# A fused conv, graph-attention and mixture-of-experts block: node degrees from a one-hot histogram, more experts and row trips ahead of the node groups

## The reference

```python
h = (x_flat @ W_gat).reshape(M, HEADS, NUM_EXPERTS)
e = leaky_relu(a_src[src] + a_dst[dst]); e_max = segment_max(e, dst)
ee = exp(e - e_max[dst]); denom = segment_sum(ee, dst)
agg = segment_sum(h[src] * (ee / denom[dst])[:, :, None], dst)
scores = layernorm(agg + b_gat).reshape(M, HEADS, NUM_EXPERTS).mean(1)
```

## Time and profile before

| | us |
|---|---|
| median of 3 runs | 2300.75 (2294.5 to 2301.59) |
| span of the profiled execution | 2297.5 |
| PE busy | 1086.1 (47%) |
| DVE busy | 1594.7 (69%) |
| ACT busy | 762.8 (33%) |
| POOL busy | 1212.5 (53%) |
| mean granted TensorE clock | 0.720 of full speed |

### The profile page before, as it was taken

How to read it: one execution, slowest core, us unless ns; L and a number is a source line. 1 busy time by engine, 2 the same in 40 slices (tenths; PEclk the granted TensorE clock), 3 DMA queues, 4 the chain that set the end, 5 groups by cost and what they waited for, 6 DMA issues and landing times. The chain is left out here.

```text
span 2297.5 us, 16425 instructions
## 1 busy us (share of the span) xinstructions
PE 1086.1 (47%) x4821; PEld 479.8 (21%) x4821; DVE 1594.7 (69%) x3100; ACT 762.8 (33%) x1260; POOL 1212.5 (53%) x1233
## 2 busy tenths in 40 slices
PE   3897878778678887000700102433342425333330
PEld 1233343334533333000300001111111112111110
DVE  6999999995726999999209504364758384747658
ACT  4664846535345554000300002222232324222221
POOL 2000000000066777777777764777777777777771
PEclk8898878787589999555855556766676768676665
DMA  8202031021454322111221611344453535363543
GB/s 297 115 1 74 1 8 38 1 8 39 47 57 110 79 71 71 14 15 29 48 41 29 43 16 41 98 144 121 121 176 85 165 92 176 72 187 73 169 113 100
DMA packets 185735, 182.76 MB, mean 80 GB/s; under 512 B 81580, under 2 KB 164462, under 8 KB 176046
## 3 DMA queue, kind: packets, MB, share of 16 engines
q1 hardware_dynamic: 99262, 88.84, 14.4%
q0 software_dynamic: 43936, 47.85, 12.4%
q10 hardware_dynamic: 42448, 45.04, 6.4%
HBM read 105.23 MB, written 76.40 MB: 79 GB/s over the span
## 5 line engine op out<-in xcount | busy, mean ns | idle before, releaser
L519 POOL DMA_INDIRECT KC<-node_dram,KB x1026 | 1018.4, 993 | 938.8 <-DMA node_dram<-node_out 626.3
L740 PE MATMUL hidden_out<-XT,W 128*128 128x512 f32 x512 | 291.3, 675 | 540.8 <-ACT ARENA_A L956 539.9
L745 PE MATMUL hidden_out<-ARENA_A,W 128*128 128x512 f32 x512 | 264.7, 642 | 24.9 <-ACT ARENA_A L956 24.9
L956 ACT ACTIVATE ARENA_A<-hidden_out,b1c 128x512 f32<-128x512 f32 x256 | 174.2, 687 | 294.5 <-PE hidden_out L740 293.9
L740 PEld LDWEIGHTS hidden_out<-XT,W 128*128 128x128 f32 x512 | 97.3, 211 | 689.5 <-ACT ARENA_A L956 570.1
L1523 DVE TENSOR_TENSOR KB<-XG,MB 128x3072 bf16<-128x3072 f32 x20 | 67.1, 3354 | 163.5 <-DMA XG<-rest_dram,win_i 100.7
L1649 DVE TENSOR_SCALAR KB<-MB 128x16 f32<-128x16 f32 (+1 forms) x33 | 5.7, 172 | 238.3 <-DMA KC<-payload,slot_idx 126.8
L1800 DVE SCALAR_TENSOR_TENSOR XG<-XT,KB,XG 128x128 f32<-128x128 f32 x512 | 144.3, 347 | 14.9 <-DMA XT<-ye_dram 11.2
L959 ACT ACTIVATE ARENA_A<-hidden_out,b2c 128x512 f32<-128x512 f32 x128 | 87.9, 687 | 185.5 <-PE hidden_out L745 185.5
L1026 ACT ACTIVATE TA<-KB 128x400 f32<-128x400 f32 x32 | 16.2, 507 | 373.3 <-DVE KB L1656 373.2
L745 PEld LDWEIGHTS hidden_out<-ARENA_A,W 128*128 128x128 f32 x512 | 98.3, 207 | 182.4 <-ACT ARENA_A L956 103.1
(11 more groups left out here) (401 smaller groups left out, 2232.0 us busy)
## 6 DMA issues: line engine op xcount, KB each, us to landing
ye_dram<-ARENA_D ACTq DMA_DIRECT2D x32, 1024.0 KB, 4.0
XT<-ye_dram SPq DMA_DIRECT2D x32, 1024.0 KB, 13.5
KC<-node_dram,KB POOLq DMA_INDIRECT x1026
payload<-XT SPq DMA_DIRECT2D x1, 11520.0 KB
payload<-KC SPq DMA_DIRECT2D x115, 90.0 KB, 1.8
XG<-x_dram SPq DMA_DIRECT2D x32, 256.0 KB, 11.3
out_dram<-XG ACTq DMA_DIRECT2D x32, 256.0 KB, 3.4
KA<-in_L_ffn_edge_index_dram SPq DMA_DIRECT2D x1, 2048.0 KB, 9.0
```

The source lines that it names most:

```text
L519: pool.indirect_dma_start(row_buf[h][:, t, :], None, node_dram, bass.IndirectOffsetOnAxis(ap=KB[:, col:col + 1].bitcast(I32), axis=0)).the ...
L740: last = pe.matmul(PF[i % 2][:, :], W1[:, m // 2, (m % 2) * P:(m % 2) * P + P], XT[:, n * CHUNK:(n + 1) * CHUNK], start=True, stop=True)
L745: last = pe.matmul(PF[i % 2][:, :], W2[:, 2 * m + kk, :], HH[:, 2 * m + kk, :], start=kk == 0, stop=kk == 1)
L956: act.activation(HH[:, m, :], PF[i % 2][:, :], ACT.Gelu, bias=b1c[:, m:m + 1]).then_inc(S["hid_out"], 1)
```

## The change

- Windows, pivots, boundaries and the storing of the lists go. `split_digits` writes each key's destination as two bfloat16 digits (node number modulo 128, and divided by 128), each twice side by side. `one_hots` compares eight columns of keys at a time with `node_iota`, a bfloat16 row in SBUF, in pairs of equal neighbours: 144 batches for list 0 (one comparison of 8 x 128 and one of 8 x 256 elements each) and 144 for list 1 (two of 8 x 128). Four buffers. TensorE adds eight products of 128 x 128 by 128 x 256 (list 1: by 128 x 128) per batch into one PSUM bank: the degrees of all nodes, with no start positions. The starts are prefix sums of the degrees (two small matmuls and a scan).
- `pick_rest` stops at the picked keys; list 1 is not sorted across partitions any more. `drop_counted` raises its keys that are not ordinary edges out of the valid range, and the rest region now begins behind list 0.
- TensorE's batches stand between the expert layers by `HOT_PLAN`: 9 batches, then three ahead of each of the 16 steps of chunks 0, 1, 2 (list 0), none in chunks 3 and 4, three ahead of each step of chunks 5, 6, 7 (list 1). 28 chunks stand ahead of the node groups. On ScalarE the exponentials of the start-up come after chunk 12, those of the rest loop after chunk 22.
- POOL: 62 early trips, the rest loop, 10 more early trips, the catch-up loop, the loop for long lists, and 42 spread trips among the node groups. 114 trips as before.

```diff
-FIRST_TRIPS = 5
-MID_TRIPS = 42
-EARLY_TRIPS = 54
+EARLY_TRIPS = 72
+REST_AFTER = 62
-SPREAD_TRIPS = 60
+SPREAD_TRIPS = 42
-AHEAD, COUNTING = 14, 2
-FIRST_CHUNKS = AHEAD + COUNTING
+FIRST_CHUNKS = 28
+HOT_BUFS, HOT_AHEAD = 4, 9
+HOT_PLAN = ((0, 3), (0, 3), (0, 3), None, None, (1, 3), (1, 3), (1, 3))
+COUNTED, STORE_REST_AT, INIT_AT, REST_AT = len(HOT_PLAN), 6, 12, 22
...
-            for trip in range(FIRST_TRIPS):
+            for trip in range(REST_AFTER):
                 gather_rows(trip)
-            gather_windows(0)
-            for trip in range(FIRST_TRIPS, MID_TRIPS):
-                gather_rows(trip)
-            gather_windows(1)
-            for trip in range(MID_TRIPS, EARLY_TRIPS):
+            steps = rest_steps(pool)
+            first = pool.value_load(rest_steps_i[0:1, 1:2], min_val=0, max_val=REST_KEYS - 1)
+            with pool.Fori(0, steps) as i:
+                fetch_rest(i, first)
+            for trip in range(REST_AFTER, EARLY_TRIPS):
                 gather_rows(trip)
...
+            def count_nodes(a, count):
+                for n in islice(batches[a], count):
+                    real = n < HOT_BATCHES
+                    pe.wait_ge(S["hot_ready"], n + 1)
+                    for t in range(HOT):
+                        last = pe.matmul(H if real else H[:, P:], hot_p[n % HOT_BUFS][:, t, :],
+                                         hot_l[n % HOT_BUFS][:, t, 0 if real else P:],
+                                         start=n == 0 and t == 0, stop=n == LISTS * HOT_BATCHES - 1 and t == HOT - 1,
+                                         skip_group_check=True)
+                    last.then_inc(S["hot_used"], 1)
...
+            def split_digits(a):
+                keys = half(KA, a).bitcast(I32)
+                link(ts(digit_i, keys, SRC_BITS, P - 1, ALU.logical_shift_right, ALU.bitwise_and))
+                link(cp(digits_p, bc(digit_i, 2, [P, LROW, 2])))
+                link(ts(digit_i, keys, SRC_BITS + 7, None, ALU.logical_shift_right))
+                link(ts(digits_l, bc(digit_i, 2, [P, LROW, 2]), float(-(KEY_BIAS // P)), None, ALU.add))
+            def one_hots(a):
+                pairs = lambda ap: ap.rearrange("p t (n e) -> p t n e", e=2)
+                for b in range(HOT_BATCHES):
+                    n = a * HOT_BATCHES + b
+                    if n >= HOT_BUFS:
+                        dve.wait_ge(S["hot_used"], n - HOT_BUFS + 1)
+                    cols = slice(b * HOT, (b + 1) * HOT)
+                    for hot, digits, low, high in ((hot_p, digits_p, 0, P), (hot_l, digits_l, (0, P)[a], 2 * P)):
+                        shape = [P, HOT, (high - low) // 2, 2]
+                        last = tt(pairs(hot[n % HOT_BUFS][:, :, low:high]),
+                                  bc(node_iota[:, low:high].rearrange("p (n e) -> p n e", e=2), 1, shape),
+                                  bc(digits[:, cols, :], 2, shape), ALU.is_equal)
+                    last.then_inc(S["hot_ready"], 1)
+                dve.wait_ge(S["hot_ready"], (a + 1) * HOT_BATCHES)
```

More of the change, by code:

```diff
@@ L733, in _, with experts @@
             last_chunk()
-            def experts(n):
+            batches = [iter(range(a * HOT_BATCHES, (a + 1) * HOT_BATCHES)) for a in range(LISTS)]
+            def count_nodes(a, count):
[8 more added lines that the diff above has]
+                    last.then_inc(S["hot_used"], 1)
+            def experts(n, beside=None):
                 done = n * len(LAYERS)
                 for i, (layer, m) in enumerate(LAYERS):
+                    if beside:
+                        count_nodes(*beside)
                     if layer == 1:
@@ L794, in _ @@
-            last.then_inc(S["boundary_ready"], 1)
+                count_nodes(a, HOT_BATCHES)
             pe.wait_ge(S["degree_ready"], 1)
-            pe.transpose(TA[0][:, 0:P], starts[:, 0, 0:P], ident[:, :])
-            pe.transpose(TA[0][:, P:2 * P], degree[:, 0, :], ident[:, :])
-            pe.transpose(TA[1][:, 0:P], degree[:, 1, :], ident[:, :]).then_inc(S["starts_turned"], 1)
+            pe.matmul(TA[0][:, 0:P], before[:, :], degree_t[:, :], start=True, stop=True)
+            pe.matmul(TA[0][:, P:2 * P], ones[:, :], degree_t[:, :], start=True, stop=True).then_inc(S["starts_summed"], 1)
@@ L1333, in quadrant_step, with sort_keys @@
                 link(stt(keys, copy, -1.0, frm, ALU.mult, ALU.min))
-            def sort_keys(which):
-                keys, copy, other = (half(k, which) for k in (KA, KB, KC))
+            def sort_keys():
+                keys, copy, other = (half(k, 0) for k in (KA, KB, KC))
                 def times_sign(col, frm=keys):
                     link(ts(keys, frm, signs[:, col:col + 1], None, ALU.mult))
-                if which:
-                    yield from row_steps(keys, other, copy)
                 for m in range(1, LEVELS + 1):
                     if m <= 4:
-                        if m > 1 or which:
+                        if m > 1:
                             times_sign(m - 1, other)
@@ new lines, in drop_counted @@
+            def drop_counted():
+                keys, flags = half(KA, 1), KC[:, 1896:1896 + LROW]
+                link(ts(flags, keys, key_bits_as_float(REAL_END), key_bits_as_float(VALID_END), ALU.is_ge, ALU.mult))
+                tt(keys, keys, flags, ALU.max).then_inc(S["rest_placed"], 1)
+            sources()
+            dve.wait_ge(S["node_out_done"], CHUNKS * GROUPS)
+            dve.wait_ge(x1_stored[3], 16 * len(x_parts[3]))
+            dve.wait_ge(S["y_ready"], NORMS)
+            link(cp(node_iota, iota_f[:, :]))
@@ new lines, in _ @@
+            split_digits(0)
+            one_hots(0)
+            sort_steps(ROW, 1)
+            split_digits(1)
+            drop_counted()
+            one_hots(1)
+            dve.wait_ge(S["hot_used"], LISTS * HOT_BATCHES)
+            cp(degree_t[:, :], H[:, 0:P]).then_inc(S["degree_ready"], 1)
+            cp(last_degree[:, :], H[:, P:])
+            dve.wait_ge(S["degree_ready"], 1)
+            red(hist_tot[:, 0:1], degree_t[:, :], AX.X, ALU.max)
+            dve.wait_ge(S["starts_summed"], 1)
```

311 lines of the change are left out of this document (61 added, 250 removed).

## The result

| | before | after |
|---|---|---|
| median of 4 runs each, us | 2298.25 (2294.5 to 2301.59) | 2263.55 (2261.97 to 2266.61) |
| span of the profiled execution | 2297.5 | 2262.1 |
| PE, DVE, POOL busy | 1086.1, 1594.7, 1212.5 | 1252.2, 1617.5, 1210.5 |
| mean granted TensorE clock | 0.720 | 0.792 |

The median before is now that of four runs; the forecast was made from three. The ratio is 0.9849, with a 95% interval from 0.9835 to 0.9864: 1.5% faster. The forecast was 2262 us. The order of reading is the same as before: POOL's waits first (waiter, releaser, us, times, longest).

What follows compares the result with a forecast made beforehand. POOL's gathers, their pitch and stops bound the kernel from 639 on. First part to 1563, plus 686.5 for the second and 9 of waits, gave 2258 us span; adding 3.25 gave 2262 us, forecast range 2235 to 2285, overall 2195 to 2305.

Steps and rivals of the forecast that it cites:

- Two elements per cycle: DVE's one-hot comparisons: 0.60 us for 1024 elements, 1.15 us for 2048, so 1.75 us per list 0 batch.
- One gather per batch in list 0: POOL beside list 0's comparisons: one gather per 1.75 us batch, 144 instead of 201.
- List 1: POOL beside list 1's comparisons: a gather every 1.30 us, 139 gathers, with the stage ending at 1115.
- The rest of the first part: POOL after the comparisons: 242 gathers at 1.25 us plus 3 us beside the start-up, 62 trips done at 1421.
- POOL's wait behind the rest loop is gone: POOL before the extra gathers: the 19.4 us wait disappears because ten trips now hide it.
- The node groups: Second part: 686.5 us, plus 9 us of POOL waits, 7 us of it where trips fall three to three groups.
- ScalarE's and PE's part: Expert chunks: 14 after 1115 end at 1378, rest loop's exponentials at 1433, six more chunks end at 1550.
- POOL isn't held: Rival, faster, chance 0.09: two-byte comparisons don't hold POOL; 57 + 5 more gathers in the stage, 77 us, 2185 us.
- One element per cycle: Rival, slower, chance 0.07: comparisons take 482 + 331 us instead of 252 + 180; 2633 us device time.
- TensorE's pace: Rival, slower, chance 0.09: TensorE at 1.2 GHz sets the stage's pace, node groups begin 90 us late, 2350 us.
- DVE as the bound in the groups: Rival, chance 0.12: POOL waits on slots in the node groups, 2295 us at the outside, 2280 likely.
- -60 windows: Ledger term for POOL's first part: removing the 48 windows saves 60 us.

Runs made afterwards that it cites:

- Experiment 1: Changed kernel with each digit read once for all its neighbours, not in pairs, so comparisons run at one element per cycle: 2642.8 us (one run).
- experiment 2: Changed kernel with the row of node numbers read as float32 from PSUM, leaving one comparison input in SBUF: 2585.8 us (one run).
- experiment 3: Changed kernel with each list 0 batch as three comparisons of 1024 elements in place of 1024 and 2048: 2236.5 us, ratio 0.9721.
- Experiments 6: Kernel before, keeping windows and sorts, with only the order of the work altered (62 early trips, rest loop, 10 more; 28 chunks ahead): 2304.4 us, ratio 1.0031.
- experiment 9: Changed kernel's histogram with the order of work of the kernel before (54 early trips, 16 chunks ahead): 2268.6 us, ratio 0.9872.
- experiment 5: Changed kernel with one spare gather behind each of the first 48 trips: 2323.7 us, ratio 1.0116.

## Why the prediction was right, and where it wasn't

The forecast (2262 us) and its main line held, each with a run behind it. That it was only 1.5 us off is partly luck. The forecast span was 2258 us and the measured one 2262.1; the 3.25 us that were added for the difference between span and median were 1.5 us in fact, and the two errors nearly cancel.

- *Two elements per cycle.* Forecast 0.60 us for 1024 and 1.15 for 2048 from start to start, after the earlier trace rows. Measured 1.74 us per batch against 1.75. The Trainium skill ("VectorE: DVE Perf Modes", section "The perf-mode tier table") gives a tensor_tensor of bf16 twice the rate of float32; the trace agrees, with 1.21 us for 2048 elements of bf16 here and 2.29 us for 2048 of float32 at L1471. Experiment 1 shows the other end of the bounds.
- *One gather per batch in list 0.* Forecast 144 by 890; measured 144 by 888.7. Experiments 2 and 3 show the reason, the second input in SBUF, from two sides.
- *List 1.* Forecast 1.30 us a gather and the stage's end at 1115; measured 1.25 and 1109. I had added 0.05 us for each gather let in. DVE does give way by some 0.05 us (a batch takes 1.25 us, twice 0.60 is 1.20), but POOL pays nothing on top: gather 316 was through at 1108. The one gather on which this step rested began, by the earlier trace rows, 0.07 us before the DVE instruction ended, not 0.04; that is a slip without weight.
- *The rest of the first part.* Forecast 3 us beside the start-up, measured 11: from 1108.0 to 1420.4 POOL takes 241 pitches of 1.296 us, not 1.25. One gather starts at 1116.69 and lasts 3.66 us:

```profile
1116.30 3.23 DVE L1342 TENSOR_TENSOR KB<-KB,down_iota 128x2944 f32<-128x2944 f32 x1
```

  That instruction has two inputs in SBUF and ends at 1119.53, 0.82 us before the gather does; it makes 2.7 of the 11 us. Three gathers from 1219.19 on (2.62, 2.02 and 2.02 us long) stand beside L1471, L1472 and L1474, with 2048 float32 elements and two inputs each: 3.8 us. The kernel before has the same three at 1312.70. The rest is mostly 2.9 us of issue ahead of the gather at 1131.07 and 1.0 us of the gather at 1114.39. The mechanism was known from the earlier trace rows, I just didn't look for it in what moved. It set off the gain of list 1, so that the end of the 62 trips came out at 1421, as forecast: partly luck.
- *POOL's wait behind the rest loop is gone.* Forecast 19.4 us, and all of them are gone: the 5.00 us that stand ahead of the extra gathers are issue, which stood ahead of the rest key's load before (5.44 us). Experiments 6 and 9 show that this term isn't a gain that stands alone.
- *The node groups.* Forecast one wait of 7 us and a few more, 9 in all; measured 7.8 once, 10.9 in all; the second part took 697.3 us against 695.5.

**A step that failed without a consequence here:** ScalarE's and PE's part. The prediction had 14 chunks follow one another after the stage and end at 1378. They ended at 1406, though the stage had ended 6 us early. After chunk 8, ScalarE does this:

```profile
1111.69 0.82 ACTq L930 DMA_DIRECT2D XG<-node_dram  x1
1112.55 13.62 ACTq L931 DMA_DIRECT2D XG<-adst_dram  x1
1126.20 11.16 ACTq L932 DMA_DIRECT2D last_row<-node_dram  x1
1137.41 1.26 ACT L885 ACTIVATE ARENA_A<-hidden_out,b1c 128x512 f32<-128x512 f32 x2 [25.76 <-issue]
```

The loads of the start-up are issued from ScalarE's queue, and the issue alone takes 25.8 us, in which no Gelu runs and PE waits. They stood in the trace of before as well (12.01 and 11.10 us, from 1267.00 on); there the 16 chunks ahead were done at 1148 and the 17th stood behind later exponentials, so they held up none. In the changed kernel the delay is hidden: ScalarE still waits 24.92 us for the rest key, and its exponentials came at 1433.7 against a forecast of 1433. But it made the price of the rival *POOL isn't held* wrong: that rival had 28 chunks ready at about 1510 and 2185 us; experiment 3, which lifts the hold, found the 28th chunk done at 1549 and 2236.5 us. Of the 39 us of the chunk some 19 come from that kernel's longer batches (its 8th chunk is stored at 1130 instead of 1111), most of the others from this issue. It was also part of what experiment 2 missed.

**The rivals.** One element per cycle costs what it was said to (experiment 1). TensorE's pace: PE had 0.99 of its clock in the stage and was busy 75%, where "70% or more" was the argument against. DVE as the bound in the groups: hardly with 42 trips and 28 chunks (10.9 us of slot waits); with 26 chunks the slot waits are 25.1 us, and with four more trips in the groups and 24 chunks 8.1. In the ledger, "-60 windows" is confirmed by experiment 5 (60.2 us), but the histogram alone brought 29 us, since the comparisons hold back gathers that the sort let through; the prediction's own terms for the two come to 60 - 35 = 25 us. From the first to the 486th row gather the kernel before took 720.0 us, for 533 pitches with the windows, and experiment 9 took 689.5 us, for 485. At 1.25 us a pitch that leaves 53.8 and 83.3 us of other time. A wait that the prediction left among its "small waits" is part of the first, and went with the windows:

```profile
POOL XG L566 <- DVEq L1525: 11.3, 1, 11.3
```

Without it 42.5 us remain for the sort's stage and what follows it, where the prediction had 43, and 83.3 for the comparisons', where it had 78: 60 + 11.3 less 40.8 is 30.5 us.

## What to carry to other kernels

When an engine that only issues is the bound, count its instructions and their pitch, and look what other engine's instructions set the pitch; here cutting one DVE instruction in two (two of 1024 elements in place of one of 2048) was worth 27 us by itself and 67 us with the order of the work fitted to it, where the whole change was worth 35. Where work is moved ahead of something, list all that each queue issues there, the DMA issues too, since 25.8 us of issue looked like nothing as long as nothing stood behind it. Test the parts of a combined change alone: the new order cost 7 us without the new algorithm and gained some 5 with it.

## What the runs showed of the hardware that was not expected

- An indirect gather on POOL that is held by a DVE instruction with two inputs in SBUF ends 0.82 us after that instruction does (0.82 beside one of 1.21 us, 0.83 beside one of 2.29 and 0.82 beside one of 3.23 us), whatever its own start. A comparison just as long with one input in PSUM doesn't lengthen it (0.94 us).
- One input in SBUF isn't always harmless. Beside this instruction, which takes 2944 elements in 1.69 us, the gather takes 1.99 us and ends 0.12 us after it:

```profile
1114.39 1.99 POOL L472 DMA_INDIRECT KC<-node_dram,KB  x1 [0.30 <-issue]
1114.57 1.69 DVE L1341 TENSOR_SCALAR KB<-KA 128x2944 f32<-128x2944 f32 x1
```

  Two more in the same trace (at 923.38 and 925.57, 1.89 us each) end 0.13 us after a CAST and a TENSOR_SCALAR with one input, of 2304 elements in 1.36 us. No experiment was made on this; why the gap is 0.13 and not 0.82 us isn't shown.
- Comparisons that start every 0.60 us, without a gap, hardly hold a gather (0.94 us, every 1.25 us); with one that takes 1.15 us in each batch, every gather is held. A gather comes round every 1.25 us at best, and then meets the end of every second short comparison.
- A bfloat16 comparison with broadcast inputs took 1.21 us for 2048 elements where two innermost neighbours are adjacent in both inputs, and 2.29 us where the innermost step of one input is zero.
